# Order inside the visits to the small tiles, maxima ahead of residuals, and an earlier q copy in a two-layer graph network on one Trainium2 core

## The reference

```python
# layer 0
Q, K, V = x @ W_q + b_q, x @ W_k + b_k, x @ W_v + b_v        # 8 heads of 64
scores = einsum('bihd,bjhd->bhij', Q, K) / 8 + gate + log(adjacency + EPS)
x = einsum('bhij,bjhd->bihd', softmax(scores), V) + x
# layer 1
scores = where(mask, -1e18, (x @ Wq + bq) @ (x @ Wk + bk).T / sqrt(512))
attn = where(mask, 0, softmax(scores))
ctx = (attn @ x) @ Wc
out = layernorm(x + ctx) * gamma + beta
```

## Time and profile before

| what | value |
|---|---|
| median of 3 runs | 2273.91 us (2271.76 to 2275.82) |
| the profiled execution | 2274.98 us, its span 2272.9 us |
| TensorE clock granted, mean | 0.996 |
| PE, DVE, ACT, POOL busy | 99%, 80%, 54%, 44% |
| DMA | 277.47 MB, 122 GB/s |

### The profile page before, as it was taken

One profiled execution on the slowest core, in us unless ns is written; L12 is line 12 of the kernel. 1 busy time (PEld: TensorE's weight loads), 2 busy tenths in 40 slices (PEclk: granted clock), 3 DMA queues, 4 the chain that ended last, 5 costly groups with the idle time before them and its releaser, 6 DMA issues.

```text
span 2272.9 us, 39420 instructions
## 1 busy us (share of the span) xinstructions
PE 2250.8 (99%) x13304; PEld 1876.3 (83%) x13304; DVE 1828.8 (80%) x5489; ACT 1219.7 (54%) x3478; POOL 991.0 (44%) x1148
## 2 busy tenths in 40 slices
PE   9999999999999999999999999999999999999997
PEld 6888888888888888888888888888888888888885
DVE  5678788788788787888888888888887878878876
ACT  5455555555455555556554555555565555555553
POOL 0154354543445443545534455435455334454334
PEclk9999999999999999999999999999999999999998
DMA  7333333334343333334333434333433333333331
GB/s 242 112 111 127 110 130 128 122 112 129 110 136 126 118 119 117 125 126 130 107 127 113 133 126 130 108 126 116 135 123 114 130 109 130 120 131 112 114 105 43
DMA packets 186586, 277.47 MB, mean 122 GB/s; under 512 B 24592, under 2 KB 122000, under 8 KB 182160
## 3 DMA queue, kind: packets, MB, share of 16 engines
q1 hardware_dynamic: 185808, 273.90, 36.6%
q10 hardware_dynamic: 576, 1.05, 0.1%
HBM read 166.28 MB, written 108.59 MB: 121 GB/s over the span
## 4 chain that ended last, share of the span: by engine, by line
PE 91%; DVE 2%; DMA 2%; POOL 1%; SPq 1%; ACT 1%; issue 1%; DVEq 0%; POOLq 0%
PE bank L245 26%; PE bank L247 25%; PE bank L246 25%; PE bank L492 5%; PE bank L528 5%; PE bank L505 5%; DVE x1n L1163 0%; DMA probsT<-turn_dram 0%; DMA gamma_b<-in_gamma 0%; DMA c_rows<-at_dram 0%; DMA turn_dram<-turned 0%; ACT probs L825 0%; POOL probs L1422 0%; DMA at_dram<-scratch 0%; ACT att L854 0%
## 5 line engine op out<-in xcount | busy, mean ns | idle before, releaser
L1422 POOL TENSOR_TENSOR probs<-probs,rcp 128x512 f32<-128x512 f32 x256 | 290.8, 1151 | 886.8 <-DVE rcp L1102 886.8
L825 ACT ACTIVATE probs<-probs,nmax 128x128 f32<-128x128 f32 x1024 | 397.3, 390 | 175.5 <-DVE nmax L1092 174.8
L1163 DVE STREAM_TRANSPOSE x1n<-x1T 32x512 f32<-32x512 f32 x496 | 348.6, 703 | 39.6 <-DMA out<-x1n 31.9
L1430 POOL TENSOR_TENSOR x_lo<-xT_land,x_hi 128x512 fp32r<-128x512 f32 x124 | 168.4, 1390 | 329.5 <-ACT x_hi L781 329.5
L1092 DVE CUSTOM_DVE_ANT_0 probs<-bank,bias 128x128 f32<-128x128 f32 x1024 | 228.5, 287 | 5.6 <-issue 2.8
L245 PE MATMUL bank<-x_hi,wk_hi 128*128 128x512 f32 x512 | 205.0, 400 | 2.2 <-DVE x_lo L1035 2.2
L809 ACT ACTIVATE k_sb<-bank,cols 128x512 f32<-128x512 f32 x128 | 88.3, 690 | 220.2 <-PE bank L247 220.2
L245 PE MATMUL bank<-x_hi,wm_hi 128*128 128x512 f32 x512 | 204.9, 400 | 0.0
L245 PE MATMUL bank<-wc_hi,x_hi 128*128 128x512 f32 x512 | 203.5, 397 | 0.0
L245 PE MATMUL bank<-wv_hi,x_hi 128*128 128x512 f32 x512 | 203.1, 397 | 0.0
L247 PE MATMUL bank<-x_hi,wk_lo 128*128 128x512 f32 x512 | 201.4, 393 | 0.0
(11 more groups left out here) (146 smaller groups left out, 5351.1 us busy)
## 6 DMA issues: line engine op xcount, KB each, us to landing
turn_dram<-turned SPq DMA_DIRECT2D x128, 512.0 KB, 2.6
probsT<-turn_dram SPq DMA_DIRECT2D x512, 128.0 KB, 2.7
xn<-in_x SPq DMA_DIRECT2D x126, 256.0 KB, 3.4
xT_land<-in_xT SPq DMA_DIRECT2D x31, 1024.0 KB, 6.9
out<-x1n SPq DMA_DIRECT2D x124, 256.0 KB, 2.0
adj_sb<-in_adj SPq DMA_DIRECT2D x32, 256.0 KB, 3.1
c_rows<-c_dram SPq DMA_DIRECT2D x32, 256.0 KB, 3.2
at_dram<-scratch SPq DMA_DIRECT2D x30, 256.0 KB, 2.0
```

The source lines that it names most:

```text
L825: op = nc.scalar.activation(probs[:, k, :], probs[:, k, :], ACT.Exp, bias=nmax[:, k:k + 1], scale=-1.0, accum_out=sums[:, k:k + 1])
L1163: op = nc.vector.transpose(x1n[b * BLK:(b + 1) * BLK, :, :] .rearrange("p g (c a s) -> p a c g s", c=C, a=P // BLK)[:, a, :, :, :], x1T[a ...
L1422: nc.gpsimd.tensor_tensor(probs[:, half, :], probs[:, half, :], rcp[:, half].unsqueeze(2).to_broadcast([P, HALF, P]), ALU.mult)\
L1430: nc.gpsimd.tensor_tensor(x_lo[:, c, :], xT_land[(t + 1) % 2][:, c, :], x_hi[:, c, :].bitcast(f32), ALU.subtract).then_inc(s["pool_x"], 1)
```

## The change

On PE the scores go ahead of probabilities times v in both visits, and the waits for the q and k copies of the same iteration that stood in front of `pv` go away (the scores wait for the same copies). On DVE the maxima of pair 0 and of pair 2 go ahead of the residuals of the neighbouring pairs. On ACT the q copy of pair 3 goes ahead of `exp1(u)`. The first step, and the last step outside `layer0_begin`, stay.

```diff
--- before.py
+++ after.py
@@ -589,14 +589,12 @@
                 project_v(t, 0)
                 pe.wait_ge(s["act_q"], nth("act_q", t, 0))
                 project_v(t, 1)
-                pe.wait_ge(s["act_k"], nth("act_k", t, 1))
-                pv(u, 2)
-                pe.wait_ge(s["act_q"], nth("act_q", t, 1))
-                pv(u, 3)
                 if w >= 0:
                     pe.wait_ge(s["dve_res"], nth("dve_res", w, 3))
                 scores(t, 0)
                 scores(t, 1)
+                pv(u, 2)
+                pv(u, 3)
                 project_v(t, 2)
                 project_v(t, 3)
 
@@ -751,13 +749,11 @@
                 project_k(t, 3)
                 pe.wait_ge(s["act_g"], nth("act_g", u, 3))
                 project_q(t, 3)
-                pe.wait_ge(s["act_k"], nth("act_k", t, 2))
-                pv(t, 0)
-                pe.wait_ge(s["act_q"], nth("act_q", t, 2))
-                pv(t, 1)
                 pe.wait_ge(s["dve_sa"], nth("dve_sa", u))
                 scores(t, 2)
                 scores(t, 3)
+                pv(t, 0)
+                pv(t, 1)
                 pe.wait_ge(s["act_k"], nth("act_k", t, 3))
                 y_whole(u, 0, STEPS)
                 pe.wait_ge(s["act_q"], nth("act_q", t, 3))
@@ -1006,8 +1002,8 @@
                 k_out(t, 2)
                 q_out(t, 2)
                 k_out(t, 3)
+                q_out(t, 3)
                 exp1(u)
-                q_out(t, 3)
                 next_x_high(it)
                 exps(t, 2, 0)
                 att1T_high(u)
@@ -1305,9 +1301,9 @@
                     next_gate(t + 1, 0)
                     next_gate(t + 1, 1)
                 bias(t)
+                maxima(t, 0)
                 residual0(u, 2)
                 residual0(u, 3)
-                maxima(t, 0)
                 x1lo(u, 2)
                 x1lo(u, 3)
                 x1_rows(u, 0)
@@ -1391,9 +1387,9 @@
                 next_gate(t + 1, 2)
                 attention1(u)
                 turn_attention(u)
+                maxima(t, 2)
                 residual0(t, 0)
                 residual0(t, 1)
-                maxima(t, 2)
                 next_gate(t + 1, 3)
                 recips(t, 2)
                 y_low(u, 0)
```

## The result

The changed kernel takes 2468.33 us (median of 4 runs, 2467.3 to 2470.15), the one before 2273.55 in the same comparison: a ratio of 1.0855 (95% interval 1.0842 to 1.0868), against a forecast of 2466. What matters is whether the parts of the sum are right too, so the same views are read again.

What follows compares the result with a forecast made beforehand. PE was taken as the bound, busy 2250.8 of 2272.9 us, so each new wait adds to the end. 2274.98 + 24.2 + 65.1 + 64.8 + 39, less 2, gave 2466 us, range 2355 to 2512.

Steps and rivals of the forecast that it cites:

- Part 1: PE's visits: still three changes of tile kind; at most some 0.2 us saved per visit, taken as zero.
- Part 2: First visit: without scores as cover, PE waits 0.78 us for the v copy, 31 times, 24.2 us.
- Part 3: ACT's q copy delays exp1 by 2.72 us; less 0.55 slack, PE waits 2.17 more at context, 65.1 in all.
- Part 4: Two of attention1's four DVE products each wait out a POOL instruction: 2.16 us more per iteration, 64.8 in all.
- (c): Rival: products slip past POOL, and PE's 2.17 us wait is too short for the clock: 2362 us, chance 0.19.
- Part 5: PE's clock falls to half in each 4.3 us wait at context: 1.3 us a fall, 39 in all.
- (b): Rival: the products meet POOL, but the clock stays at full: 2427 us, chance 0.20.
- Part 6: DVE's maxima ahead of residuals: what waits for residuals has over 2 us of room, so no cost.
- 2 us taken off the sum: PE's existing waits for a DMA, which the scores now cover: 2 us less.
- (d): Rival: not slower; change from scores to probabilities times v is free, saving 12 us: 2263, chance 0.02.
- (e): Rival: the change doesn't do what it says and the time stays, chance 0.01.
- (f): Rival: slower still, three products caught and 2.3 us for each clock fall: 2528 us, chance 0.08.

Runs made afterwards that it cites:

- split visit: Kernel before, first visit reordered to scores of pair 0, both halves of probabilities times v, scores of pair 1: 2281.76 us, ratio 1.0033.
- POOL held: Changed kernel, with POOL's residuals x_lo held until attention1's products and transpose are over: 2359.93 us, ratio 1.0378.
- filled wait: Changed kernel, with 12 matmuls into a bank nobody reads put ahead of PE's wait for att1T_lo: 2417.19 us, ratio 1.0632.
- first maxima alone: Kernel before, with only the maxima of pair 0 ahead of the residuals, PE's visits in their old order: 2287.04 us, ratio 1.0072.
- run of the first visit: Kernel before, with only the first visit (scores first) and the maxima of pair 0 as in the changed kernel: 2297.75 us, ratio 1.0105.
- second visit alone: Kernel before, with only the second visit (scores first) and the maxima of pair 2 as in the changed kernel: 2272.39 us, ratio 0.9995.
- q copy alone: Kernel before, with only ACT's q copy of pair 3 moved ahead of exp1: 2441.28 us, ratio 1.0742.

## Why the prediction was right, point by point

**Part 1, the order in a visit: right.** The second visit takes 4.201 us in either order, so the change that was in no row is not free; a fourth change costs 0.198 us in the split visit. Zero was the right choice within the bound.

**Part 2, the v copy's cover: right.** 0.78 forecast, 0.77 measured; 24.2 against 23.75 us.

**Part 3, exp1 behind the q copy: right in place, too high in size.** Exp1 starts 0.59 behind the q copy as forecast, but the stretch from the transpose to att1T_high, which is two DMAs, took 5.37 us instead of 5.84 on the mean. The shift at context is 2.72 - 0.48 - 0.55 = 1.69, where 2.17 was forecast: 51 for 65.1. "Each link waits for the one before, so the shift is carried to the end" took the DMAs as rigid, and they were not; quicker DMAs were one of the signs of being wrong that the prediction named. With POOL held the term can be read alone: the wait at context grew by 55.5 us (56.6 less 1.1), with 5.50 us from the transpose to att1T_high.

**Part 4, the meeting with POOL: right.** Two caught of four, 30 of 30, 2.06 against 2.16 us: 62 for 64.8. That the offset of a single row of bias could be carried over was the risk, and rival (c), products that slip past, is excluded. Holding POOL back undoes the loss. Parts 3 and 4 together gave 1.69 + 2.06 = 3.75, and the standstill grew by 113.3 / 30 = 3.78.

**Part 5, the clock: right in mechanism, too low in size.** Forecast 1.3 us a fall, 39; measured 1.7 a fall and 51 us by the filled wait. The middle between nothing and 2.3 was the term mis-sized: the fall comes from 1.5 us before PE's return to 1.2 behind it, so most of it is paid. Rival (b), a clock that stays up, is excluded; the filled wait makes its case, 51 us away from what happened.

**Part 6, the rest: right for this change, and not in general.** "DVE is not PE's partner there" is false by itself: the first maxima alone cost 13.9 us, most of it by making exp1 late. It costs nothing here because the scores go ahead too, as the run of the first visit shows. The 2 us taken off the sum are not shown: the second visit alone was 1.3 us faster, which its interval does not tell from nothing.

**The sum.** Span against span the loss is 193.6 us: 113.3 of context's wait, 23.8 of v copies, 52 of the clock by distances (51 by the filled wait), and 3 for the longer first distance behind 30 waits, a term that the sum did not have. That leaves 1 to 2 without a place. Forecast were 129.9, 24.2, 39, and 2 taken off. That the sum met the result to 2 us is luck: two errors, 17 too much for the wait and some 13 too little for the clock, cancel. The mechanisms are shown; the sizes were good to about 15 us, not to 2.

**The rivals.** Holding POOL makes the case of (c): 2359.93 where 2362 was worked out for it, and here too a shorter wait (55.5 for 65.1) and some falls of the clock that (c) did not have partly cancel. (d) is excluded by the second visit alone, which gains nothing by its order, and by the q copy alone; (e) by the time; (f) by the count of two products and 1.7 us a fall.

## What to carry to other kernels

An engine with slack may still stand at the head of a chain that the bound engine waits for, so an instruction moved ahead of another in its queue must be priced by what it itself waits for: the q copy is 0.69 us long and cost 168 us, since its input came 2.1 us after exp1 could start, and since what it held back then met POOL and let the clock fall. Where such a shift brings a product of DVE with two operands in SBUF behind the start of a POOL instruction, count whole POOL instructions. Where the clock falls behind a wait, the wait costs nearly half as much again (3.8 us of waiting and 1.7 for the clock here). And the price of one reordering depends on the others: the first maxima cost 13.9 us alone, and nothing once the scores of their visit go first.

## What the runs showed of the hardware

The clock's fall behind a standstill did not come every time. Behind 3.8 us it fell in 30 of 30 iterations of the changed kernel, and in 24 of 30 in the profile of the q copy alone (the six without a fall had 3.3 to 3.8 us). In the kernel with POOL held, 1.89 us on the mean, it fell in 3 of 30, behind 1.99, 2.69 and 3.08 us; with the first maxima alone once, behind 2.00 us; and with the 12 added matmuls, 1.15 us, never. What decides it was not tried.

The DMAs of the chain were quicker at their new moment: from the transpose to att1T_high 5.37 instead of 5.84 us on the mean, and less scattered: the shortest is 5.3 in both, the longest 5.6 instead of 7.1. The return from DRAM (at_dram into c_rows) before, then in the changed kernel:

```profile
DMA to landing us min/median/max: 1.8/2.0/3.8
...
DMA to landing us min/median/max: 1.8/1.9/2.1
```

With POOL held, where the chain starts 2.72 us later than before, the stretch is 5.50 us on the mean. Whether another transfer shared their time before was not tried, and the cause stays open.

One more change of the kind of tile on PE cost 0.198 us a visit (4.399 for 4.201), and a visit with three changes took 4.201 us whether scores or probabilities times v came first. The distance between starts at a change is 0.20 us out of scores or probabilities times v, into any other kind, and 0.32 out of a projection, whose usual distance is 0.227.
